# Top-32 selection of one and a quarter batches moved into the loop before it

## Time and profile before

| | us |
|---|---|
| median of 3 runs (3417.8 to 3423.83) | 3422.09 |
| profiled execution | 3416.65 |
| its span | 3414.9 |
| memory loop, turns 0 to 7 | 540.23 to 676.57 |
| memory loop, turn 8, and opening | 676.57 to 708.11 |
| selection of batch 0 | 708.11 to 752.69 |
| selection of batch 1 | 752.69 to 807.88 |
| selection of batch 2 | 807.88 to 866.26 |
| selection of batch 7 ends | 1157.20 |

### The profile page before, as it was taken

The page is one execution under the profiler, slowest core; times in us unless marked ns, Lnnn a source line. Parts: engine busy times, 40 slices in busy tenths (PEclk is TensorE's granted clock), DMA queues, the critical chain, the costliest instruction groups (busy, mean ns, idle before and its releaser), DMA issues.

```text
span 3414.9 us, 52169 instructions
## 1 busy us (share of the span) xinstructions
PE 3007.4 (88%) x20631; PEld 2000.8 (59%) x20671; DVE 1882.4 (55%) x6414; ACT 1240.9 (36%) x1935; POOL 437.5 (13%) x456
## 2 busy tenths in 40 slices
PE   5999999938889778876888789989899999998888
PEld 3666667825555445554555555656567666666653
DVE  4434343379989525664467786756333344434445
ACT  1222222324555433221333356854333233233443
POOL 0010101113333210000001034620000000000000
PEclk9999999968999899987999878999899999999999
DMA  3000000010000010000000001100000000000000
GB/s 119 1 1 1 1 1 1 1 49 1 1 1 1 23 38 1 1 1 5 1 1 1 9 18 33 26 38 1 25 1 0 1 1 0 1 1 1 9 1 25
DMA packets 21725, 37.75 MB, mean 11 GB/s; under 512 B 2085, under 2 KB 19686, under 8 KB 20457
## 3 DMA queue, kind: packets, MB, share of 16 engines
q1 hardware_dynamic: 20664, 34.02, 2.9%
q10 hardware_dynamic: 816, 0.39, 0.0%
HBM read 26.81 MB, written 2.10 MB: 8 GB/s over the span
## 4 chain that ended last, share of the span: by engine, by line
PE 68%; DVE 22%; ACT 5%; issue 3%; SPq 1%; POOL 0%; DMA 0%; DVEq 0%; ACTq 0%; POOLq 0%
PE ps L382 39%; DVE arena L533 4%; DVE arena L1816 4%; PE ps L579 2%; DVE arena L1807 2%; PE ps L2891 2%; PE ps L2200 2%; PE ps L2910 2%; PE ps L626 2%; PE ps L2154 2%; PE ps L481 2%; ACT arena L614 2%; PE ps L667 2%; PE ps L1499 1%; PE ps L518 1%
## 5 line engine op out<-in xcount | busy, mean ns | idle before, releaser
L382 PE MATMUL ps<-weights,arena 128*128 128x256 f32 (+4 forms) x2480 | 698.9, 432 | 21.8 <-ACT arena L1633 6.1
L382 PE MATMUL ps<-arena,weights 128*128 128x256 f32 (+4 forms) x1726 | 570.7, 480 | 38.9 <-DMA fp_bias<-in_fp_bias 27.2
L382 PEld LDWEIGHTS ps<-weights,arena 128*128 128x128 f32 (+1 forms) x2480 | 468.0, 199 | 184.5 <-issue 97.2
L382 PEld LDWEIGHTS ps<-arena,weights 128*128 128x128 f32 (+1 forms) x1726 | 324.3, 196 | 246.3 <-issue 153.4
L382 PE MATMUL ps<-arena 128*128 128x256 f32 (+4 forms) x1618 | 428.4, 418 | 5.2 <-ACT arena L4348 1.5
L382 PEld LDWEIGHTS ps<-arena 128*128 128x128 f32 (+2 forms) x1618 | 300.5, 189 | 115.3 <-issue 75.3
L614 ACT ACTIVATE arena<-ps 77x2048 f32<-77x2048 f32 (+1 forms) x112 | 210.0, 1875 | 171.4 <-PE ps L579 154.3
L533 DVE TENSOR_REDUCE arena<-ps 128x16 f32<-128x1232 f32 (+2 forms) x96 | 179.1, 1866 | 149.2 <-PE ps L518 49.7
L1816 DVE MATCH_REPLACE8 arena<-arena 128x77 f32<-128x77 f32 x1024 | 215.1, 227 | 0.0
L2167 ACT ACTIVATE arena<-ps 128x1536 f32<-128x1536 f32 x128 | 185.7, 1452 | 73.0 <-PE ps L2156 66.5
L795 POOL TENSOR_TENSOR x<-x,weights 128x512 f32<-128x512 f32 x32 | 43.8, 1370 | 1276.6 <-DVE arena L761 1263.6
(11 more groups left out here) (408 smaller groups left out, 4503.9 us busy)
## 6 DMA issues: line engine op xcount, KB each, us to landing
arena<-arena SPq DMA_DIRECT2D x156, 32.0 KB
weights<-in_w_L_attn SPq DMA_DIRECT2D x1, 4608.0 KB, 19.2
weights<-in_w_L_ffn SPq DMA_DIRECT2D x1, 3848.0 KB, 11.5
weights<-in_w_L_xattn SPq DMA_DIRECT2D x3, 1024.0 KB, 6.3
weights<-in_w_L_ffn SPq DMA_DIRECT2D x1, 3072.0 KB, 9.9
x<-in_x SPq DMA_DIRECT2D x1, 2048.0 KB, 8.3
weights<-in_w_L_xattn SPq DMA_DIRECT2D x1, 2048.0 KB, 7.4
out<-x SPq DMA_DIRECT2D x8, 256.0 KB, 2.2
```

The costliest lines, as they stand in the source:

```text
L382: ins = k.nc.tensor.matmul(out, lhsT, rhs, start=start and i == 0, stop=i == n - 1)
```

## The change

Batch 0's whole selection and the first 64 slots of batch 1's (320 slots) are issued by VectorE in turns 4 to 8 of the memory loop, 64 a turn, in parts of 24, 8, 16 and 16 slots: behind hidden 0, behind hidden 1, behind the addition of b2, behind hidden 2. What they need moves there too: the constants, layer norm constants of tiles 0 to 3 and z of batches 0 and 1 (VectorE, turn 3), keys and values (TensorE, turns 1 and 2), transposes and queries (turns 3 and 5), scores (turns 3, 4, 6, 8), the transposed first maxima (turn 7), the copies and masks on ScalarE, the bias of values and x on GpSimd. The layer norm constants of the other 12 tiles are made after the loop.

To leave banks 4 to 7 to the scores, the memory loop lives on banks 0 to 3: hidden i goes to bank 2 + i % 2, and both gates to bank 1 beside out. So hidden 2 waits for VectorE to have read hidden 0 of its own turn, hidden 3 for hidden 1, hidden 0 and 1 for hidden 2 and 3 of the turn before; gate 1 waits for the addition of b2, gate 2 for gate 1's sigmoid, out 0 for gate 2's sigmoid of the turn before. The memory loop's signals get semaphores of their own. The tiles of L0 xattn are laid out anew in the arena. Behind the loop there is no opening: TensorE makes the kept scores of batch 0, waits for the expert weights, and enters the selection loop at turn 1; VectorE enters at slot 64 of batch 1.

```diff
+    e, l = Carve(k.arena, k.arena_size, FREE), Carve(k.arena, k.arena_size)
...
 def L0_selected_tensor(k, pe, s):
-    enter(k, pe, s.sig)
-    first = s.steps[0]
-    turned_z_tensor(k, pe, s, first, 3)
-    context_kv_tensor(k, pe, s, first, 2)
-    after(pe, s, first, "zT")
-    query_tensor(k, s, first, s.zT, 3)
-    after(pe, s, first, "q")
-    after(pe, s, first, "k")
-    all_scores_tensor(k, pe, s, first, 0)
-    after(pe, s, first, "left", 1)
-    all_scores_tensor(k, pe, s, first, 1)
+    after(pe, s, s.steps[1], "left", 2)
+    kept_scores_tensor(k, pe, s, s.steps[0], 0)
+    kept_scores_tensor(k, pe, s, s.steps[0], 1)
+    pe.wait_ge(*s.behind.memory.at("g2", 0, B - 1, 1))
     pe.wait_ge(*k.loaded["L0_ffn"])
-    for n in range(B + 1):
+    for n in range(1, B + 1):
...
+SELECT_FROM, SELECT_PARTS = 4, (24, 8, 16, 16)
+SELECTED = (B + 1 - SELECT_FROM) * sum(SELECT_PARTS)
+
+def early_selection_vector(k, dve, s, n, part):
+    start = (n - SELECT_FROM) * sum(SELECT_PARTS) + sum(SELECT_PARTS[:part])
+    for at in range(start, start + SELECT_PARTS[part]):
+        selection_vector(k, dve, s, at // 256, at % 256)
+
+def L0_selected_vector(k, dve, s):
+    k.nc.vector.memset(s.f.keys, BIG)
+    norms_part_vector(k, dve, s.norms, 1)
+    for n in range(SELECTED // 256, B):
+        for at in range(SELECTED % 256 if n == SELECTED // 256 else 0, 256):
+            selection_vector(k, dve, s, n, at)
+            between_vector(k, dve, s, n, at)
...
 def memory_hidden_tensor(k, pe, s, n, i):
-    if n:
-        pe.wait_ge(*s.memory.at("mT", 0, n - 1, i + 1))
+    if i >= 2:
+        pe.wait_ge(*s.memory.at("mT", 0, n, i - 1))
+    elif n:
+        pe.wait_ge(*s.memory.at("mT", 0, n - 1, i + 3))
...
 def L0_attn_tensor(k, pe, s):     # memory loop, turn n, step i
+            if i == 1 and n in (3, 5):
+                turned_z_tensor(k, pe, one, one.steps[n // 2 - 1], 4)
+            if i == 2 and n == 7:
+                after(pe, one, one.steps[1], "left", 1)
+                turn_tops_tensor(k, pe, one, one.steps[0], HI, 3 * P)
             if i < 2:
                 memory_out_tensor(k, pe, s, last, i)
+            if i == 0 and n == 4:
+                all_scores_tensor(k, pe, one, one.steps[0], 1)
+            if i == 1 and n in (3, 5):
+                query_tensor(k, one, one.steps[n // 2 - 1], one.zT, 6)
+            if i == 3 and n == 1:
+                context_kv_tensor(k, pe, one, one.steps[0], 5)
+            if i == 3 and n == 2:
+                context_kv_tensor(k, pe, one, one.steps[1], 7)
+            if i == 3 and n in (3, 6):
+                all_scores_tensor(k, pe, one, u, 0)
+            if i == 0 and n == 8:
+                all_scores_tensor(k, pe, one, one.steps[1], 1)
...
 def L0_attn_vector(k, dve, s, x_loaded, const_loaded, n_const):     # memory loop
             if n < B:
                 memory_hidden_vector(k, dve, s, n, i)
+            if n == 3 and i == 0:
+                norms_part_vector(k, dve, one.norms, 0)
+                turned_z_vector(k, dve, one, one.steps[0], None)
+            if n == 3 and i == 2:
+                turned_z_vector(k, dve, one, one.steps[1], None)
+            if n >= SELECT_FROM and i < 2:
+                early_selection_vector(k, dve, one, n, i)
             if last is not None and i == 1:
...
+            if n >= SELECT_FROM and i in (1, 2):
+                early_selection_vector(k, dve, one, n, i + 1)
```

More of the change, by code:

```diff
@@ L106 @@
           "probT_v", "o_ps", "raw", "back_ps", "o", "oT_ps", "oT", "out_ps", "ctx")
+MEMORY = ("m_ps", "m_sg", "mT", "swaT_ps", "swaT", "om_ps", "om", "omT_ps", "omT", "g1_ps", "g1", "g2_ps", "g2", "gated",
+          "merged", "part", "stats")
 class SignalPool:
@@ L118, in called @@
             return name
-        if stage == "L2_attn" or name.startswith(("early_", "g_")):
+        if stage == "L2_attn" or name.startswith(("early_", "g_")) or (stage == "L0_attn" and name in MEMORY):
             return f"{name}_of_{stage}"
@@ L1316, in selected_plan @@
 def selected_plan(k):
[L1318 to L1325, removed]
+    e, l = Carve(k.arena, k.arena_size, FREE), Carve(k.arena, k.arena_size)
+    s = Bag(stage="L0_xattn", norms=norms_plan(k, "L0_xattn", 4), zT=e.take(KC, SEQ), qT=[e.take(KC, SEQ) for _ in (0, 1)],
+            kT=[e.take(KC, 2 * CTX) for _ in (0, 1)], v=[e.take(1, H, VW) for _ in (0, 1)],
+            left=[e.take(4, 4 * CTX) for _ in (0, 1)], top=e.take(2, 16, 8), later=e.take(16, 8), kb=e.take(KC, 2),
+            big=e.take(1), minus=e.take(P, dt=BF16), rest=e.take(2, 4, 4), rec=e.take(2, H))
+    s.drop = [e.take(4, 4 * CTX, dt=BF16), Carve(k.arena, k.arena_size, BIAS_ROWS).take(4, 4 * CTX, dt=BF16)]
+    s.prob = l.take(4, 4 * SEQ)
+    l.at = Z_MEMORY
+    s.z = [l.take(2, D) for _ in (0, 1)]
+    s.parts, s.mT = l.take(2, 4, PAD, dt=BF16), l.take(SEQ, dt=BF16)
+    c = l
+    s.raw, s.o, s.oT = c.take(4, SEQ), c.take(2, D), c.take(KC, SEQ)
     s.f = Bag(st=c.take(2, 6), mv=c.take(2, 2), var=c.take(2), rstd=c.take(2), t=c.take(2), z=c.take(2, D),
@@ L1603, in L0_selected_scalar @@
     a = k.nc.scalar.activation
[L1604 to L1614, removed]
+    for r in (0, 1):
+        turned_probs_scalar(k, act, s, s.steps[0], r)
+    for n in range(1, B + 1):
         now, last, _, soon, _ = neighbours(s.steps, n)
@@ L1789, in L0_selected_vector @@
         .then_inc(*s.setup.up("ready"))
[L1790 to L1819, removed]
@@ new lines, with selection_vector @@
+SELECT_FROM, SELECT_PARTS = 4, (24, 8, 16, 16)
+SELECTED = (B + 1 - SELECT_FROM) * sum(SELECT_PARTS)
+def selection_vector(k, dve, s, n, at):
+    u, t, i, r = s.steps[n], at // 128, at // 32 % 4, at % 32
+    half, h = r // 8 % 2, r % 8
+    left, tops = of_half(s, t, half)[:, h, :], tops_of_half(s, t, half, i)[:, h, :]
+    if r < 16:
+        if r == 0 and i == 0:
+            after(dve, s, u, "left", t + 1)
+            if n and t == 0:
+                dve.wait_ge(*s.sig.at("x_part", 0, n - 1, 2))
+        if h == 0:
+            if i:
+                after(dve, s, u, "cut", 8 * t + 2 * i + half - 1)
+            hold(k, dve, "vector")
+        ins = k.nc.vector.max(tops, left)
+        if h == 7:
+            ins.then_inc(*s.sig.up("x_max"))
+    else:
+        if h == 0:
+            after(dve, s, u, "max", 8 * t + 2 * i + half + 1)
+            hold(k, dve, "vector")
+        ins = k.nc.vector.match_replace(left, tops, left, -BIG)
+        if h == 7:
+            ins.then_inc(*s.sig.up("x_cut"))
@@ L1848, in L0_selected_gpsimd @@
             later_z_gpsimd(k, pool, s, later, now)
-        if now:
+        if n and now:
             split_tops_gpsimd(k, pool, s, now)
@@ L3047, in memory_out_tensor @@
         if n:
-            pe.wait_ge(*s.memory.at("om", 0, n - 1, 1))
+            pe.wait_ge(*s.memory.at("g2", 0, n - 1, 1))
     ins = proj_token(k, k.ps[:, 1, t * D:(t + 1) * D], s.mT[n % 2], t * P, s.w2, None, HID // P)
@@ L3165, in L0_attn_tensor @@
     pe.wait_ge(*s.update.at("db", 0, 0, 2))
+    one = s.ahead
     for n in range(B + 1):
@@ L3220, in L0_attn_scalar @@
     act.wait_ge(*s.update.at("db", 0, 0, 2))
+    one = s.ahead
+    u, v = one.steps[0:2]
+    k.nc.scalar.activation(one.minus, k.identb[:, :], ACT.Copy, scale=-1.0)
     for n in range(B + 1):
@@ L3227, in L0_attn_scalar @@
                 continue
+            if i == 0 and n in (2, 3):
+                act.wait_ge(*one.setup.at("ready", 0, 0, 1))
+                context_kv_scalar(k, act, one, one.steps[n - 2], 1 + 2 * n, True)
+                context_kv_scalar(k, act, one, one.steps[n - 2], 1 + 2 * n, False)
+            if i == 1 and n == 4:
+                left_scalar(k, act, one, u, 1)
+            if i == 1 and n in (3, 5):
+                turned_z_scalar(k, act, one, one.steps[n // 2 - 1], 4)
+            if i == 0 and n in (6, 8):
+                drop_scalar(k, act, one, u, n // 2 - 3)
+            if i == 0 and n == 7:
+                left_scalar(k, act, one, v, 0)
+            if i == 3 and n == 7:
+                turn_tops_scalar(k, act, one, u, HI, 3 * P)
+            if i == 1 and n == 8:
+                left_scalar(k, act, one, v, 1)
             if i == 1:
@@ L3230, in L0_attn_scalar @@
                 k.nc.scalar.activation(flat(s.swaT), k.ps[:, 0, :], ACT.Copy).then_inc(*s.memory.up("swaT"))
+            if i == 2 and n in (3, 5):
+                query_scalar(k, act, one, one.steps[n // 2 - 1], 6)
             if i == 2:
@@ L3241, in L0_attn_scalar @@
                     act.wait_ge(*s.memory.at("done", 0, last - 1, 1))
-                k.nc.scalar.activation(flat(s.g2), k.ps[:, 3, :], ACT.Sigmoid).then_inc(*s.memory.up("g2"))
+                k.nc.scalar.activation(flat(s.g2), k.ps[:, 1, :], ACT.Sigmoid).then_inc(*s.memory.up("g2"))
+            if i == 3 and n == 3:
+                left_scalar(k, act, one, u, 0)
 def bias_rows_vector(k, dve, s):
@@ L3331, in L0_attn_vector @@
     dve.wait_ge(*s.update.at("db", 0, 0, 2))
+    one = s.ahead
```

(10 more changed lines are left out.)

44 lines of the change are left out of this document (26 added, 18 removed).

## The result

The changed kernel takes 3367.79 us, median of 4 runs (3365.22 to 3368.27), against 3420.89 for the kernel before on the same chip (3417.8 to 3423.83): ratio 0.9843, 95% interval 0.9826 to 0.9860. It is 53 us faster; 51 were forecast (3371, range 3360 to 3386).

The account below looks back on a forecast made before the run. PE was taken to bound the memory loop, VectorE the selections behind it. With the added costs and waits, batch 1's mask moves from 807.9 to 756.9, 51.0 us: 3422.1 - 51 = 3371 us, range 3360 to 3386.

Parts of the forecast that it names:

- The parts fit: Turns 4 to 8 of the memory loop: 55.6 us of selection fits VectorE's idle gaps, costing 0.
- Fewer banks: Memory loop on shared banks: margin gone only at the loop's start, costing 0.5 us.
- PE's added work: Memory loop up to turn 8: keys, values, queries, transposes, scores and waits delay turn 8 by 12.2 us.
- The last x: Turn 8: the last x is ready 16.35 us behind the turn's start, at 705.1.
- The wait for the weights: Behind the loop: PE passes the expert-weight wait at 717.5, 12.4 us behind x; VectorE waits 3.1 us before the mean.
- Rival 3: Behind the loop: no expert-weight wait and PE at its higher clock, 5 us less, 3366 us; chance 0.06.
- From the mean on: Selection loop: mean to residual 6.9 us, residual to batch 1's mask 27.55, then 58.4 a turn as before.
- Rival 1: Memory loop: the parts don't fit, 2 to 3 us in each of four turns, 3381 us; chance 0.15.
- Rival 2: Turns 3 to 5: GpSimd blocks two VectorE instructions a turn, 5 us, 3376 us; chance 0.06.
- Rival 4: Selection turn 1: the weight wait delays the expert chain, giving back another 6 us, 3377 us; chance 0.04.
- Rival 5: Memory loop: the parts stand wholly in PE's way, all 55.6 us exposed, 3427 us; chance 0.03.

Follow-up runs that it names:

- e2: The changed kernel with the same 64 slots of a turn issued in one part behind hidden 0: 3390.61 us, against 3417.67 for the kernel before.
- e3: The kernel before with only the memory loop's move to four shared PSUM banks: 3420.72 us against 3417.67, ratio 1.0007.
- e6: Changed kernel with the expert-weight wait moved to turn 1's first router product, 80 slots a turn, batch 0's mean before slot 144: 3364.75 us, before 3417.11.
- e1: The changed kernel with TensorE's expert-weight wait moved from before turn 1 to its first router product: 3362.20 us (again 3359.27), changed kernel 3369.95.
- e4: The changed kernel with all 320 early slots and their dependents issued behind the memory loop: 3418.39 us against 3417.67 before, ratio 1.0005.

## Why the prediction was right

**The parts fit: right.** 0 was taken for 55.6 us of added VectorE work. Turns 4 to 7 show no wait of PE at all. e2 shows that this is the fit and not the total. e6 shows PE waiting 4.2 us in two turns when each turn gets 16 more slots.

**Fewer banks: one place of two.** 0.5 us was taken, all of it at the loop's start; e3 shows 0.24 there and 0.78 at out 0 of turn 8, which the prediction didn't have. Together 1.0 us, too little to be told in the time.

**PE's added work: 12.2 us forecast, 10.4 measured.** Turn 8's first matmul is at 684.30 - 537.55 = 146.75 instead of 136.34. Part of this is the clock: before, the loop began at the lower level (0.64 granted from 540.23 to 545.0, 80 matmuls in 19.57 us against 18.27 after), so the like-for-like figure is about 11.7. That includes the 1.0 us of waiting for banks. The work alone was counted too high: the next instruction starts before the end of the one in front, so queries cost 1.74 and not 1.89 each (596.55 to 598.29), transposes 0.44 and not 0.60, scores 0.74 and not 0.81, 0.8 us in all; and PE's wait for z in turn 3, taken at 0.6, shows no bracket.

**The last x: right.** 16.45 us behind the start of turn 8 (700.06 + 0.69), with 16.35 forecast.

**The wait for the weights: right in place, too small in size.** Forecast were PE passing it 177.3 us behind the loop's start, and VectorE waiting 3.1 us at the mean. Measured are 176.5 and 5.55 (6.52 on PE). The size is off since VectorE came 1.7 us earlier than forecast (at 714.91, 177.4 behind the loop's start, instead of 719.3 - 540.2 = 179.1) and PE needed from the outputs to the mean 720.46 - 714.06 = 6.4 instead of 4.9 us. The 4.9 came from the earlier trace rows, where the first 16 matmuls took 1.28 us and the transposes back 1.09; behind the idle 6.52 us all ran at 1.2 GHz (0.50 granted), 3.62 us for 32 and 1.91 for the transposes. This step of the forecast, the 4.9, was mis-sized by 1.5 us. e1 shows the price of the wait: 5.6 us up to the mean. Rival 3 had 5.

**From the mean on: right.** 34.0 us to the mask (34.5 forecast), then 58.39 a batch; D fell by 50.8, with 51.0 forecast.

**How much of the match is luck.** From the loop's start the last x came 1.7 us earlier than forecast, the way from there to the mean took 2.4 us more, and the way on to the mask 0.5 less. That these add up to 0.2 is luck, and the kernel before was 1.3 us longer by its clock, which no term of the forecast holds. The mechanism is not luck: e4, e2 and e1 each change one part of it and move the time as the account says.

**The rivals.** Rival 1 (the parts don't fit) didn't come about at 64 slots; at 80 it begins to, in turn 8 above all. Rival 2: one product (L3417) took 0.82 instead of 0.69 us in turn 4 beside GpSimd's bias. The trace agrees with the rule from the Trainium skill (SBUF — State Buffer, Who interferes with whom): this product has two SBUF inputs, and it is the only one in turns 3 to 5 that runs beside a GpSimd instruction, for 0.3 us. The price was 0.13 us, not 5. The two engines meet at a price at z of the second layer norm, behind the residual: 2.39 us after, 2.37 before, so that drops out of the difference. The 16 replaces of turn 6 between 660.44 and 663.68, with GpSimd's products at 661.09 and 662.26 beside them, took 3.24 us where 3.23 had been worked out: one input, no loss, as the rule has it. Rival 4: ScalarE's idle time before the mask is 0.96 us as before, nothing given back. Rival 5: e2 is the nearest to it and shows its mechanism, a part in the wrong place, at 24 us.

Open is why the memory loop starts up to 6 us apart in profiles of one and the same kernel. A lower granted clock from 50 to 100 us goes with it; what sets it in one execution and not in another no run tells.

## What to carry to other kernels

In this kernel 55.6 us of an idle engine's work went beside a loop that another engine bounds and made no turn from 4 to 7 wait, since it was cut to the idle gaps of the turn and kept what frees a bank in front; the same work in one piece gave back 24 us of the 51. What it needs from the bounding engine (10.4 us here) is not free. Read the gaps from the brackets of one turn's timeline, and add up the parts from the same trace. When an opening is taken away, look for what it had hidden (here a weight load tied to the last x), and put that wait in front of the first user, not in front of the loop.

## What was not expected of the hardware

PE's waits of 3.5 to 5.6 us cost more than themselves: the eight gate matmuls behind each took up to 3.75 us instead of 1.97, at a granted clock of 0.50 to 0.52, so e2's 17.2 us of added waiting became 24. Behind waits of 1.84 and 2.71 us the clock stayed at 1.00.

Two VectorE instructions of one SBUF tensor each (z of two tiles) took 2.32 to 2.45 us when a GpSimd instruction began at most 0.40 us behind their start, and 0.73 to 0.74 when it began later. A move of a few tenths in GpSimd's start was worth 1.7 us on the path, about as much as 10 slots.
